# A two-stage attention kernel: making a branch flag ahead of the change of stage, and projecting cross queries from split operands

## What is computed

```python
h = _layernorm(x, ln1_g, ln1_b)
x = x + _mha(h, h, sa_wq, ...)            # self attention, 2048 keys
h = _layernorm(x, ln2_g, ln2_b)
x = x + _mha(h, context, ca_wq, ...)      # cross attention, 1601 keys
h = _layernorm(x, ln3_g, ln3_b)
h = gelu(h @ mlp_w1.T + mlp_b1) @ mlp_w2.T + mlp_b2
return x + h
```

## Time and profile before

| | us |
|---|---|
| median of 3 runs | 1455.71 (1455.01 to 1456.9) |
| the profiled execution | 1458.83 |
| its span, first to last instruction | 1457.2 |
| PE busy, share of the span | 94% |
| ACT busy, share of the span | 75% |
| DVE busy, share of the span | 41% |
| mean granted clock of TensorE | 0.975 |

### The profile page before, as it was taken

The page is one execution under the profiler, slowest core; times in us unless marked ns, Lnnn a source line. Parts: engine busy times, 40 slices in busy tenths (PEclk is TensorE's granted clock), DMA queues, the critical chain, the costliest instruction groups (busy, mean ns, idle before and its releaser), DMA issues.

```text
span 1457.2 us, 20715 instructions
## 1 busy us (share of the span) xinstructions
PE 1373.8 (94%) x8014; PEld 631.9 (43%) x8014; DVE 590.9 (41%) x1377; ACT 1086.6 (75%) x1357; POOL 47.5 (3%) x70
## 2 busy tenths in 40 slices
PE   7999989998779999999999999999999999999977
PEld 5667766786432223223322322332334333433437
DVE  5646676677740204313332331342441243144232
ACT  3543434455459999999999999799888788788843
POOL 2010000001010000000000000000000000000000
PEclk9999999999979999999999999999999999999998
DMA  9410001001268100000010353601000000000000
GB/s 306 164 47 1 1 0 58 1 1 53 72 164 119 31 23 13 27 27 14 12 52 14 46 107 62 158 30 37 24 12 16 23 12 12 23 15 1 5 11 15
DMA packets 35044, 66.00 MB, mean 45 GB/s; under 512 B 6202, under 2 KB 20092, under 8 KB 34204
## 3 DMA queue, kind: packets, MB, share of 16 engines
q1 hardware_dynamic: 29580, 43.24, 13.1%
q0 software_dynamic: 5360, 21.37, 4.1%
HBM read 42.70 MB, written 22.02 MB: 44 GB/s over the span
## 4 chain that ended last, share of the span: by engine, by line
PE 79%; ACT 10%; DVE 7%; issue 3%; DMA 0%; DVEq 0%; SPq 0%; ACTq 0%
PE PS L1474 27%; PE PS L1457 20%; ACT PX L1008 7%; PE PS L1556 2%; PE PS L1524 2%; PE PS L1244 2%; PE PS L1247 2%; PE PS L1206 2%; PE PS L1257 2%; PE PS L1207 2%; PE PS L1208 1%; PE PS L1505 1%; PE PS L1071 1%; PE PS L1539 1%; PE PS L1507 1%
## 5 line engine op out<-in xcount | busy, mean ns | idle before, releaser
L1008 ACT ACTIVATE PX<-PS 128x1024 f32<-128x1024 f32 (+1 forms) x928 | 869.9, 1108 | 99.8 <-PE PS L1457 77.5
L1474 PE MATMUL PS<-PX,V 128*32 128x512 f32 (+1 forms) x3712 | 498.8, 609 | 5.5 <-ACT PX L1008 4.0
L1457 PE MATMUL PS<-QST,stack 50*128 50x512 f32 (+1 forms) x1856 | 375.5, 467 | 12.1 <-ACT PX L1008 7.2
L1457 PEld LDWEIGHTS PS<-QST,stack 50*128 50x128 f32 (+1 forms) x1856 | 155.1, 184 | 391.4 <-ACT PX L1008 354.2
L1474 PEld LDWEIGHTS PS<-PX,V 128*32 128x32 f32 (+1 forms) x3712 | 74.0, 108 | 153.5 <-issue 130.9
L2139 DVE COPY OT<-PS 128x512 f32<-128x512 f32 x32 | 22.1, 692 | 214.1 <-PE PS L1474 213.3
L836 ACT ACTIVATE PH<-PS 128x512 fp32r<-128x512 f32 (+1 forms) x52 | 31.2, 600 | 82.8 <-PE PS L1187 73.0
L2174 DVE RECIPROCAL REC<-REC 128x256 f32<-128x256 f32 x30 | 52.6, 1753 | 1.0
L1556 PE MATMUL PS<-W,HIDT 128*128 128x256 f32 x192 | 44.6, 385 | 4.6 <-ACT HIDT L991 4.6
L854 ACT ACTIVATE TR<-PS,small 128x128 f32<-128x128 f32 x32 | 10.0, 364 | 51.2 <-PE PS L1247 51.2
L1866 DVE TENSOR_TENSOR PL<-PEXP,PH 128x512 fp32r<-128x512 f32 (+1 forms) x52 | 35.8, 689 | 28.0 <-ACT PEXP L837 27.2
(11 more groups left out here) (220 smaller groups left out, 1565.7 us busy)
## 6 DMA issues: line engine op xcount, KB each, us to landing
QST<-q_parts SPq DMA_DIRECT2D x192, 64.0 KB
q_parts<-PARTS POOLq DMA_DIRECT2D x16, 512.0 KB, 3.6
stack<-k_parts SPq DMA_DIRECT2D x24, 200.1 KB, 6.8
stack<-k_parts SPq DMA_DIRECT2D x18, 256.0 KB
k_parts<-KPARTS POOLq DMA_DIRECT2D x8, 512.0 KB, 3.2
v_cross<-V POOLq DMA_DIRECT2D x1, 3328.0 KB, 12.1
V<-v_cross SPq DMA_DIRECT2D x2, 1664.0 KB, 13.3
k_parts<-PARTS POOLq DMA_DIRECT2D x6, 512.0 KB, 3.3
```

Source lines behind the costliest of these rows:

```text
L1008: act.activation(exp_place(a, h)[0:kr, :, :], PS[0:kr, slot:slot + 2, :], ACT.Exp, scale=SCALE).then_inc(at["exp"], 1)
L1457: ins = pe.matmul(PS[0:kr, score_slot(a, h) + jj, :], KST[a][lo:lo + NROW, pair, kt * P:kt * P + kr].bitcast(F32R), QST[lo:lo + NROW, pair ...
L1474: ins = pe.matmul(PS[32 * j:32 * j + 32, 6, :], V[0:kr, kt, 2 * (g // 2 * GH + j) + g % 2, :], exp_place(a, 2 * (c * steps + t) + j // 2)[ ...
```

## The change

Three things change.

First, flag 1 is made at step 59 of the last self chunk and PE loads it at step 61 (`FLAG_STEP`, `FLAG_LOAD`). PE loads flag 2 three steps ahead of the first cross chunk's end. The branches stay where they are. The last `pv` of the self stage is issued after the first scores of the cross stage. SP loads the values of groups 2 and 3 after `general(1)` instead of ahead of it.

Second, `u` uses split operands as `m` does. DVE splits `CAWQ` once (event `wq`, step 20 of the first self chunk) and splits `HC` in every chunk; `HCH0` moves to a place that is free in the self stage too.

Third, each unit of `u` is whole in one step (27 and 40; 20 and 22 in the first cross chunk) and `n` is whole in step 54.

```diff
-    {"y": [5, 8, 11, 14], "h": [19, 22], "u": [25, 28, 38, 41], "n": [54, 57]},
+    {"y": [5, 8, 11, 14], "h": [19, 22], "u": [27, 27, 40, 40], "n": [54, 54]},
-LAST_REST = {"y": [5, 7, 9, 11], "h": [16, 17], "u": [19, 19, 21, 21], "n": [30, 30], "flag": [36], "w1": [42, 45]}
+LAST_REST = {"y": [5, 7, 9, 11], "h": [16, 17], "u": [20, 20, 22, 22], "n": [30, 30], "flag": [36], "w1": [42, 45]}
+FIRST_REST = {"wq": [20]}
+FLAG_STEP, FLAG_LOAD = 59, 61
...
+    CAWQL = m.put("CAWQL", [P, 2, D], F32, oCAWQ)
+    CAWQH = m.put("CAWQH", [P, 2, D], F32, oON + GP * CHUNK * 4 + CHUNK * 4)
...
+        if a == 0 and c == CHUNKS - 1:
+            ev[FLAG_STEP].append((0, "flag", 0, 0, True))
...
-                sp.wait_ge(A[0]["pv"], HALVES // 2)
+                load_values(GROUPS - 1, HALVES // 2)
                 sp.dma_start(W1[:], d["w1T"].rearrange("(c p) n -> p c n", p=P)).then_inc(S["w1_loaded"], 16)
...
-            def general(f):
+            def load_flag(f):
+
+                pe.wait_ge(A[DECIDES[f][0]]["flag"], decision(f)[2])
+                return pe.value_load(flag[0:1, f:f + 1], min_val=0, max_val=1)
+
+            def general(f, bounded):
...
-            decide(a)
-            general(a)
+            if a == 0:
+                decide(0)
+                general(0, load_flag(0))
+            else:
+                general(1, bounded)
...
-            def hidden(out_, i, c, span):
+            def hidden(kind, out_, i, c, span):
                 w = slice(i * P, (i + 1) * P)
-                hi, lo = W1H[c][:, w].bitcast(F32R), W1L[:, c, w].bitcast(F32R)
+                if kind == "u":
+                    hi, lo = CAWQH[:, c, w].bitcast(F32R), CAWQL[:, c, w].bitcast(F32R)
+                else:
+                    hi, lo = W1H[c][:, w].bitcast(F32R), W1L[:, c, w].bitcast(F32R)
...
             def chunk(c, first):
+                    if a == 0 and c == CHUNKS - 1 and t == FLAG_LOAD:
+                        loaded = load_flag(1)
+                    if a == 1 and first and t == GROUPS * NK - 3:
+                        loaded = load_flag(2)
                     if t == 0:
+                        if a == 1 and first:
+                            self_pv(CHUNKS - 1, GROUPS * NKS[0] - 1)
                         if not first:
                             pv(c - 1, steps - 1)
                         scores(c, 1, first)
...
-            pv(CHUNKS - 1, steps - 1)
             if a == 0:
+                self_pv = pv
                 continue
+            pv(CHUNKS - 1, steps - 1)
...
             def piece(kind, i, q, a=a, at=at):
+                if kind == "wq":
+                    ve.wait_ge(S["saw_loaded"], 64)
+                    ch(ve.tensor_copy(CAWQH[:].bitcast(F32R), CAWQ[:]))
+                    ve.tensor_tensor(CAWQL[:].bitcast(F32R), CAWQ[:], CAWQH[:], ALU.subtract) \
+                        .then_inc(S["wq_split"], 1)
...
-                    if a == 1:
-                        ch(ve.tensor_copy(HCH[i][:].bitcast(F32R), HC[:, i, :]))
-                        ve.tensor_tensor(HCL[:, i, :].bitcast(F32R), HC[:, i, :], HCH[i][:], ALU.subtract) \
-                            .then_inc(at["hc_lo"], 1)
-                        ve.wait_ge(at["hc_lo"], 2 * q + i + 1)
+                    ch(ve.tensor_copy(HCH[i][:].bitcast(F32R), HC[:, i, :]))
+                    ve.tensor_tensor(HCL[:, i, :].bitcast(F32R), HC[:, i, :], HCH[i][:], ALU.subtract) \
+                        .then_inc(at["hc_lo"], 1)
+                    ve.wait_ge(at["hc_lo"], 2 * q + i + 1)
```

More of the change, by code:

```diff
@@ L189, in build @@
     R = s.new("R", [HEADS, CHUNK], F32)
-    CAWQ = s.new("CAWQ", [P, 2, D], F32)
+    oCAWQ = s.region(2 * D * 4)
+    CAWQ = m.put("CAWQ", [P, 2, D], F32, oCAWQ)
+    CAWQL = m.put("CAWQL", [P, 2, D], F32, oCAWQ)
+    CAWQH = m.put("CAWQH", [P, 2, D], F32, oON + GP * CHUNK * 4 + CHUNK * 4)
+    assert GP * CHUNK * 4 + CHUNK * 4 + 2 * D * 4 <= GROUPS * CHUNK * 4
     NQ = m.put("NQ", [P, CHUNK], F32, oQST + 7 * CHUNK * 4)
@@ L428, in wait_parts_stored, with events @@
             eng.wait_ge(S[f"{kind}parts_stored{mm}"], 16 * n)
-    def events(a, first):
+    def events(a, first, c):
         NK = NKS[a]
@@ L562, in load_shift, with load_values @@
                         .then_inc(s_to, 16)
+            def load_values(g, last):
+                sp.wait_ge(A[0]["pv"], last)
+                sp.dma_start(V[:, 0:LT, (g - 1) * GH:(g + 1) * GH, :],
+                             vd.rearrange("p (k h e) -> p k h e", k=LT, h=HEADS)
+                             [:, :, (g - 1) * GH:(g + 1) * GH, :]).then_inc(s_vst[g // 2], 16)
             if a == 0:
@@ L601, in _ @@
                     load_shift(0, g, s_qst[1][g])
[L602 to L607, removed]
+                    if g == 1:
+                        load_values(g, last)
             def general(f):
@@ L1430, in general, with scores @@
                     pe.sem_inc(at["decided"], 1)
-            decide(a)
-            general(a)
-            def scores(c, n, first):
+            if a == 0:
[3 more added lines that the diff above has]
+                general(1, bounded)
+            def scores(c, n, first, a=a, at=at, NK=NK, steps=steps):
                 h = c * steps * 2 + n
@@ L1460, in scores, with pv @@
                 ins.then_inc(at["scores"], 1)
-            def pv(c, t):
+            def pv(c, t, a=a, at=at, NK=NK, steps=steps):
                 g, kt = t // NK, t % NK
@@ L1533, in piece @@
                     ins.then_inc(at["hT"], 1)
[L1534 to L1543, removed]
+                if kind in "um":
+                    if kind == "u" and i == 0 and first:
+                        pe.wait_ge(S["wq_split"], 1)
                     if first:
@@ L1546, in piece @@
                     for c in share(2):
-                        ins = hidden(PS[:, 7, :], i, c, slice(0, CHUNK))
+                        ins = hidden(kind, PS[:, 7, :], i, c, slice(0, CHUNK))
                     if last:
@@ L1590, in chunk @@
                         scores(c, 2 * t + 3, first)
-            chunk(0, True)
+                return loaded
+            bounded = chunk(0, True)
             if a == 1:
-                general(2)
+                general(2, bounded)
                 pe.wait_ge(S["w1_split"], 2)
@@ L1597, in _ @@
             for c in range(1, CHUNKS):
-                chunk(c, False)
+                bounded = chunk(c, False)
+            if a == 0:
+                self_pv = pv
+                continue
             pv(CHUNKS - 1, steps - 1)
-            if a == 0:
-                continue
             sums(CHUNKS, 0)
@@ L2291, in chunk @@
             def chunk(c, first):
-                ev = events(a, first)
+                ev = events(a, first, c)
                 for t in range(GROUPS * NK):
```

45 lines of the change are left out of this document (23 added, 22 removed).

## The result

The changed kernel took 1451.01 us (median of 17 runs, 1446.81 to 1453.83), the kernel before 1455.71 (17 runs). The ratio is 0.9963, with a 95% interval of [0.9953, 0.9974]: 5.4 us faster, 3.8 to 6.8. The ratio is estimated from the single runs; the two medians alone lie 4.70 us apart, a quotient of 0.9968. The profiled execution took 1447.71 us with a span of 1446.0.

A forecast was written before the change was run, and what follows sets the result against it. ACT's exponentials bound the kernel; PE work costs only the gaps it leaves there. Terms -4.8 + 0 + 0.1 - 0.7 = -5.4 us on 1458.83 gave 1453.4, ratio 0.9963; scaled to the median, 1450.5, range 1448.0 to 1453.4.

The forecast's parts named there:

- The change of stage, -4.8: Self to cross stage: flag made ahead and last pv behind first scores make it like a chunk change, saving 4.8 us.
- The branch: PE's branch at the change of stage: 0.33 us, taken as hidden behind the last but one pv; 0.4 us if uncovered.
- Flag 2, 0: PE's earlier load after the first cross chunk, with redrawn clock falls: counted 0, bounds -2.6 to +1.3 us.
- Cross queries in the self stage, +0.1 for six: Six units of u, split operands, whole in one step: +0.1 us together, between -1.3 and +2.0.
- Cross queries in the first cross chunk, -0.7: Two units of u there, whole before too, now with split operands: 2 x -0.34 = -0.7 us.
- Norms, DVE's splits, SP: 0: Whole norms on PE, 10 us of splits on DVE and SP's later load of values: each expected to cost 0.
- The clock falling at the new change of stage: Rival: PE's short idle spells there lower the clock, costing 1.3 us; time 1451.7, chance 0.17.
- The stall at step 61: Rival: PE reaches step 61 before the flag is there and stalls; gain -1 or so, 1455 us, chance 0.05.
- the late values: Rival: values of groups 2 and 3 land after step 26 needs them at 971; slower from 976 on, chance 0.04.
- the dearer units: Rival: whole units of u leave gaps of 0.91 and 0.29; +2.0 in the self stage, 1452.6 us, chance 0.13.
- The saving of 0.53 a unit in full: Rival: PE bounds around u, so each unit saves 0.53 us; sum -9.0, time 1446.7, chance 0.04.
- The sum: Whole kernel: the terms add to -5.4 us, ratio 0.9963, predicted time 1450.5 us.

The follow-up runs named there:

- flag_only: The change with only its flags, last pv and SP's order; cross queries from float32 operands in the old steps: 1453.45 us, ratio 0.9983 to the kernel before.
- f32_whole: The change, but cross queries from float32 operands, still a unit whole in one step: 1455.44 us in one run.
- halves: The change, but each unit of u in two halves again, in both stages, and n in two steps: 1450.44 us, ratio 0.9956 to the kernel before.
- best: The change, but units of u in two halves in the self stage only, n whole: 1450.24 us, ratio 0.9947 to the kernel before.
- filler: The change plus two unused matmuls in PE's idle spell at cross-stage chunk changes and the change of stage: 1449.83 us, ratio 0.9943 to the kernel before.
- whole_again: The change, unedited, run again on another chip: 1449.43 us, ratio 0.9956 to the kernel before.
- load_late: The change, but PE loads both flags only at the branch, though they are made early: 1450.20 us, ratio 0.9951 to the kernel before.
- best_filler: The change with self-stage units of u in halves and the two unused matmuls at chunk changes: 1449.52 us, ratio 0.9940 to the kernel before.
- thirds: The change, but self-stage units of u in three shares, three steps apart: 1449.67 us, ratio 0.9956 to the kernel before.
- pv_first: The change, but the self stage's last pv issued ahead of the branch and first cross scores, as before: 1453.39 us, ratio 0.9985 to the kernel before.

## Why the prediction was right

The predicted 1450.5 and the ratio of 0.9963 agree with 1451.01 and 0.9963 (0.9968 by the medians). The mechanism at the change of stage was right; that the sum fits so closely is in part luck, as the last point says. Point by point:

**The change of stage, -4.8.** In flag_only the two chunks that hold it are 4.97 us shorter. (The timed runs of flag_only give only 2.5 for the whole kernel, with falls of the clock elsewhere.) The mechanism came as foretold in each part: the gap of an ordinary change of chunk, no stall at step 59 or 61, the clock held. Undoing parts gives the shares: the order of the last `pv` 0.9, the flag ahead with SP's order 4.1 by subtraction, and within that the early load 0.3, where I had priced an uncovered load at 0.5. PE's queued `pv` covers the branch, but not the load and the branch together.

**The branch.** It lies behind `pv`. The rule of the Trainium skill (Runtime: NRT & Kernel Launch, instruction fetch mechanics) about a stall at a taken branch shows in no profile here: the branch lasts 313 to 374 ns in all twelve, and even with the load in front of it PE idled 0.25 us and no more.

**Flag 2, 0.** Before, PE idled 0.20 us at this load and branch, more than the third of 0.31 that I had read there. The second cross chunk lasts 127.34 us after and 128.53 before. The third, whose start has no branch, lasts 127.37. So the branch costs nothing, and the 1.2 us between 128.53 and 127.34 were the clock's fall, which this execution does not have.

**Cross queries in the self stage, +0.1 for six.** Measured about -0.25: 123.15 a chunk against 123.24 in flag_only, three times. The free margin was mis-sized. It is 0.63 us in terms of the visible gap where a piece has another shortly before it (0.90 leaves 0.27, 1.06 leaves 0.43), and 0.73 behind a long row of steps (1.60 leaves 0.87, 1.91 leaves 1.18). I had taken one margin from the closely spaced halves. That 0.53 us less of PE work a unit hardly reaches the time is right, but it is the sum of two effects that I had not separated. The split operands by themselves save 0.30 to 0.32 us a unit (f32_whole against the change, flag_only against halves). Putting the unit whole into one step loses 0.27 again (halves against the change), because the margin is had once and not twice.

**Cross queries in the first cross chunk, -0.7.** 104.26 in flag_only, 103.76 in the change: -0.5. The gaps were 0.85 and 0.74, from 1.07 and 1.06; the first lies between the two values that I had named, 0.73 and 0.91.

**Norms, DVE's splits, SP: 0.** No wait of `u` for DVE's low parts, nor of PE for stacks or values, shows. Whole norms cost nothing (best against halves). In halves, though, DVE's copy of the heads was late and cost 1.09 us in one place: the cover there is thin. SP issued the values at 917.17, which is 920.9 on the old kernel's scale, slightly ahead of the 921 to 923 foretold.

**The rivals.** The clock falling at the new change of stage: in none of the eleven profiles with the change or a variant of it. A profile shows one execution, so how often it falls there in the timed runs is not known. The rule of the Trainium skill (TensorE: Matmul & The Clock Gate, "A second HAM failure mode: psum-queue depth-cycling") says that frequent micro-idles can make the clock swing. The trace agrees in that the clock still falls at some changes of chunk, where PE idles 0.31 and 0.65 us; filler shows that filling the second of these does not stop it. The stall at step 61, the late values, the dearer units: refuted by the profile. The saving of 0.53 a unit in full: refuted by self chunks of 123.15 against 123.24, 0.05 a unit.

**The sum.** It agrees better than its parts deserve. The profiles from the self stage on differ by 7.4 us (1031.7 before, 1024.3 after), of which 5.6 lie in the two chunks at the change of stage, 0.2 in the other two whole self chunks, 0.3 in the first, and 1.2 in a fall that the one execution had and the other had not. Over many runs the falls that go seem to be partly replaced by others.

## What to carry to other kernels

Make a branch's flag, and load it, some steps ahead of the place where the program turns on it, and let the engine issue the next stage's first work ahead of the last stage's last. Where a second engine is the bound, a piece of work on the first costs what of it sticks out of its lead. Less work in a piece gains that much, and putting two pieces together loses it again; cut the work into pieces which the lead covers, and see that the engine that takes the result is not made late. In a kernel whose clock falls here and there, compare stretches of profiles, and read a timed difference of a few us together with the mean clock of the runs.

## What was not expected of the hardware

The clock of TensorE falls to 0.50 for 3.41 or 6.83 us at starts of cross chunks, where PE waits for ACT only a few tenths of a us, and which of them it is goes with shifts of a few us elsewhere: behind the start of the second and the fourth cross chunk in the kernel before, f32_whole and halves, of the fourth alone in the change, whole_again, load_late and filler, and of the third in best, best_filler, thirds, pv_first and flag_only, the last two with another fall within the second cross chunk. In best, whose self stage is 1.6 us shorter than the change's, a fall of 6.83 us stands in the third cross chunk in place of one of 3.41 in the fourth; it cost 2.8 us and the other 1.35. Filling most of an idle spell of 0.65 us did not avert a fall. What decides it is open.
